# A decoder layer on one core: state and retrieval of its delta-rule recurrence in 32x32 blocks of TensorE

## The chip, the cores and the metric

The kernel runs on one core of a Trainium2 chip. The metric is the time of one execution on the device, in microseconds (us). Before the change the median of three runs is 969.68 us (969.55 to 969.97).

## The reference, cut to what matters

A pre-norm decoder layer over x of 8 x 512 x 256: first a recurrent ("delta rule") attention with 16 heads of 16 features, then attention over a context, then a feed-forward block with quantised activations (8 bits, scaled by the 0.995 quantile of the absolute values) and ternary weights. The change concerns the recurrence and, at the end, the second quantile.

```python
def step(S, inp):
    q_t, k_t, v_t, beta_t = inp
    retrieval = jnp.einsum('bhij,bhj->bhi', S, k_t)
    S = S + jnp.einsum('bhi,bhj->bhij', beta_t * (v_t - retrieval), k_t)
    o_t = jnp.einsum('bhij,bhj->bhi', S, q_t)
    return (S, o_t)
_, out_t = lax.scan(step, S0, (q, k, v, beta))
...
amax = jnp.maximum(jnp.quantile(jnp.abs(x), 1.0 - 0.005), EPS)
```

S is one 16 x 16 matrix for each of 8 batch rows and 16 heads, 128 matrices in all.

## The kernel before

**Stages.** After a start of some 40 us the recurrence runs in 32 chunks of 16 tokens (`CT`, `NCK`), until about 620 us; then the attention over the context, the feed-forward block's upper product, the second quantile (`quantile(1, ...)`) and the lower product. Everything is in one program, in which each engine's queue is written out by hand; semaphores tie them together. The steps of a chunk j appear in the order in which the `for j in range(NCK + 1)` loop of each engine calls them.

**The loop from chunk to chunk.** Within a chunk the update vectors of 16 tokens depend on each other. VectorE solves this triangular system (`solve(j, ...)`, some 30 small operations) and then transposes the update vectors (`updates_turned`, L1344, two halves, semaphore `ut_ready`). TensorE adds the chunk's outer products to the state (`state`, L1933). The state stays in one PSUM bank, `psS`, accumulated over all chunks. It is copied to SBUF, TensorE multiplies it with the keys and queries of the next chunk (`retrieval`, L1971, semaphore `ret_mm`), and VectorE starts the next chunk's right side from that (`start_chunk`, L1427) and solves again.

**Blocks and zeros.** A partition of these tiles is a batch row and a token (keys, updates) or a batch row and a feature (state). Every product is block-diagonal: 8 batch rows of 16 partitions. The 32x32 transposes of VectorE give tiles in which two batch rows share a 32-block; the kernel before spreads them into full 128x128 operands with zeros around the blocks:
- `keys_spread` on ScalarE (L725, four copies a chunk) spreads the turned keys `kt` into `kexp`, of which `state` takes 8 matrices of 128x128 as stationary operands against 64 columns each.
- `state` on ScalarE (L698, eight copies of 32 partitions, the lower two blocks, in two halves by heads, semaphore `sexp_act`) and `state` on VectorE (L1412, four masked products, the upper two blocks, `sexp_dve`) spread the state into `sexp`, of which `retrieval` takes one 128x128 matrix for each head, 16 in all, against up to 96 columns: 32 of its own head's and, on either side, columns that lie between and meet zeros in `padded`.

A matmul in f32 appears in the trace as two passes, each a weight load (PEld) and a matmul (PE); so `state` is 16 passes a chunk and `retrieval` 32. The word pass is used in this sense below.

**What stands between them on TensorE.** Between `state` and `retrieval` TensorE does a transpose of the next inputs (L2068), `values` (L2024) and `updates_turned` (L1943), 12 passes. After `retrieval` come the key sums (L2033), `far_gram` (L1956), `attention` in products of 32 rows by 128 columns (L1994), `outputs` in products of 128 rows by 32 columns (L2046), and then projections and the near grams, up to the next `state`.

**Who waits for what.** TensorE's sequencer executes a semaphore instruction of its own when a matmul has more waits than one; these appear in the trace as EVENT_SEMAPHORE (PEldq), at L1932 before `state` (for `ut_ready`) and at L2066 behind it (for the next transpose). ScalarE copies the attention products out (L733), which frees their banks.

**The second quantile.** `narrowed(1, ...)` compares 2048 candidates a partition with 4 edges: three marks by VectorE in bf16 (L1682), counted by TensorE (edges 0 and 2, L2282) and by ScalarE (edge 1, L1160), and the fourth marked and counted by VectorE alone (L1683). Then the candidates under a bound are kept: 1280 columns by VectorE (L1704), 768 by GpSimd (L682, L684), and VectorE takes the 8 largest of each 64 (L1709).

## Time and profile before

| | before |
|---|---|
| median of 3 runs | 969.68 us (969.55 to 969.97) |
| the profiled execution, its own time | 975.51 us |
| its span, first to last instruction | 973.6 us |
| TensorE (PE) busy | 861.1 us, 88% |
| VectorE (DVE) busy | 822.7 us, 85% |
| ScalarE (ACT) busy | 699.3 us, 72% |
| GpSimd (POOL) busy | 523.5 us, 54% |
| mean granted clock of TensorE | 0.950 of full speed |

PE is TensorE's matmuls, PEld its weight loads, and L12 is line 12 of the kernel. A row of the timeline is a group of like instructions in a row: when the first started, how long from there to the end of the last, and how many. The ends of matmuls are modelled and overlap the next start, so intervals between starts are used for how long a group holds TensorE. A granted clock of 1.00 is 2.4 GHz, and 0.50 is 1.2 GHz; a value between them is a mean over a stretch with both.

### The profile page before, as it was taken

The numbers are of one execution on the slowest core, as the hardware profiler recorded it, in microseconds if no ns is written. First come the engines' busy times: TensorE is split into PE (matmuls) and PEld (weight loads), VectorE is DVE, ScalarE is ACT, GpSimd is POOL, SyncE is SP. The second block draws the span as 40 slices with busy tenths as digits, with TensorE's granted clock in tenths as the row PEclk, the third lists the DMA queues.
The fourth block names the chain that finished last, engine by engine and source line by source line (L and its number), as shares of the span: only waits on it lengthen the run. The fifth ranks groups of instructions, "written<-read, shape, count | busy, mean of one in ns | idle before, by whom it ended". The sixth has DMA issues, their size and how long they took to land.

```text
span 973.6 us, 19722 instructions
## 1 busy us (share of the span) xinstructions
PE 861.1 (88%) x6257; PEld 657.5 (68%) x6257; DVE 822.7 (85%) x2508; ACT 699.3 (72%) x1819; POOL 523.5 (54%) x501
## 2 busy tenths in 40 slices
PE   7899999999999999999999999879999813995285
PEld 6687887787787787787787777556666513443264
DVE  4789999989999999999999988756777787899797
ACT  4688888887788788788778766536777750895095
POOL 5446656665465565565455544445888860980100
PEclk9899999999999999999999999989999965998599
DMA  9900000000000000004000000133110000000023
GB/s 162 159 1 13 7 7 13 6 7 12 7 8 11 8 7 11 8 7 140 8 8 10 9 6 8 36 132 130 66 66 0 2 1 0 1 1 1 0 68 106
DMA packets 28573, 30.50 MB, mean 31 GB/s; under 512 B 5548, under 2 KB 23864, under 8 KB 28472
## 3 DMA queue, kind: packets, MB, share of 16 engines
q1 hardware_dynamic: 28256, 29.12, 11.9%
q8 instruction: 51, 0.84, 0.4%
q14 instruction: 50, 0.41, 0.1%
q10 hardware_dynamic: 216, 0.14, 0.1%
HBM read 20.85 MB, written 4.19 MB: 26 GB/s over the span
## 4 chain that ended last, share of the span: by engine, by line
PE 65%; ACT 15%; DVE 12%; issue 6%; POOL 1%; DMA 1%; ACTq 0%; POOLq 0%; DVEq 0%
PE ps L2002 10%; PE ps L1933 5%; PE psY L1971 5%; PE psX L1971 4%; PE ps L2118 4%; PE psG L1956 4%; PE ps L1994 4%; ACT arena L733 3%; PE psG L1950 3%; PE ps L2060 3%; PE psX L2139 3%; PE psY L2139 2%; PE ps L2325 2%; PE psG L1951 2%; ACT arena L698 2%
## 5 line engine op out<-in xcount | busy, mean ns | idle before, releaser
L523 POOL TENSOR_SCALAR_AFFINE_SELECT arena<-arena 128x2048 f32<-128x2048 f32 x32 | 64.5, 2015 | 163.3 <-DVE arena L1308 163.3
L538 POOL TENSOR_TENSOR work<-work,half 128x16 f32<-128x16 f32 x32 | 94.9, 2966 | 2.7
L527 POOL TENSOR_SCALAR_AFFINE_SELECT arena<-arena 128x2048 f32<-128x2048 f32 x32 | 92.1, 2879 | 2.2
L698 ACT ACTIVATE arena<-ps,nparity 32x128 f32<-32x128 f32 x248 | 76.2, 353 | 18.8 <-PE ps L1933 17.3
L1994 PE MATMUL ps<-work 32*128 32x256 f32 x512 | 82.6, 402 | 3.0 <-ACT arena L733 2.9
L733 ACT ACTIVATE arena<-ps 128x512 f32<-128x512 f32 x128 | 69.3, 593 | 16.6 <-PE ps L1994 15.8
L1994 PEld LDWEIGHTS ps<-work 32*128 32x128 f32 x512 | 53.5, 184 | 37.3 <-issue 28.3
L1327 DVE TENSOR_REDUCE arena<-arena 128x64 f32<-128x256 f32 (+1 forms) x96 | 65.9, 687 | 3.3
L1971 PE MATMUL psY<-work,arena 128*128 128x96 f32 (+1 forms) x512 | 61.7, 280 | 3.1 <-ACT arena L698 2.0
L1971 PEld LDWEIGHTS psY<-work,arena 128*128 128x128 f32 x512 | 60.0, 196 | 6.5 <-issue 6.5
L537 POOL TENSOR_SCALAR work<-work 128x16 f32<-128x16 f32 x32 | 8.1, 254 | 102.1 <-ACT work L750 102.1
L1956 PE MATMUL psG<-arena 128*128 128x512 f32 x128 | 62.7, 612 | 0.0
L1933 PEld LDWEIGHTS ps<-work,arena 128*128 128x128 f32 x496 | 58.2, 192 | 5.2 <-issue 3.5
L1933 PE MATMUL ps<-work,arena 128*128 128x64 f32 x496 | 59.4, 273 | 0.5 <-DVE work L1344 0.5
L1971 PEld LDWEIGHTS psX<-work,arena 128*128 128x128 f32 x480 | 54.7, 192 | 4.6 <-issue 4.6
L1971 PE MATMUL psX<-work,arena 128*128 128x96 f32 (+1 forms) x480 | 56.3, 276 | 1.5 <-ACT arena L698 0.3
L2002 PEld LDWEIGHTS ps<-arena 128*128 128x128 f32 x384 | 48.1, 196 | 9.4 <-ACT arena L733 4.6
L1412 DVE TENSOR_TENSOR arena<-ps,arena 32x256 f32<-32x256 f32 x124 | 51.4, 414 | 3.5 <-PE ps L1933 1.2
L2002 PEld LDWEIGHTS ps<-nT,arena 128*128 128x128 f32 x384 | 46.3, 191 | 9.3 <-ACT arena L733 4.1
L2002 PE MATMUL ps<-arena 128*128 128x128 f32 x384 | 51.2, 284 | 0.9
L725 ACT ACTIVATE arena<-work 32x256 f32<-32x256 f32 x124 | 51.0, 411 | 1.1
L2002 PE MATMUL ps<-nT,arena 128*128 128x128 f32 x384 | 49.3, 279 | 2.1 <-ACT nT L787 1.2
(362 smaller groups left out, 2498.1 us busy)
## 6 DMA issues: line engine op xcount, KB each, us to landing
arena<-in_mask_BxSxS_ik SPq DMA_DIRECT2D x8, 1024.0 KB, 6.7
xs<-arena SPq DMA_DIRECT2D x256, 16.0 KB, 1.8
arena<-in_ctx SPq DMA_DIRECT2D x8, 512.0 KB, 4.2
out<-xs SPq DMA_DIRECT2D x32, 128.0 KB, 1.7
arena<-in_x SPq DMA_DIRECT2D x8, 288.0 KB, 17.5
arena<-in_L_ffn_w SPq DMA_DIRECT2D x2, 1024.0 KB, 20.6
arena<-in_x SPq DMA_DIRECT2D x16, 96.0 KB, 6.6
arena<-in_L_attn_w_qkvb SPq DMA_DIRECT2D x2, 512.0 KB, 5.9
```

The source lines that it names most:

```text
L523: G.affine_select(out=keys, in_=keys, compare_op=ALU.is_ge, fill=0.0, base=0, pattern=[[0, NH], [1, P]], channel_multiplier=-1).then_inc(h ...
L527: G.affine_select(out=pairs, in_=pairs, compare_op=ALU.is_ge, fill=0.0, base=0, pattern=[[0, NH], [-CT, B], [0, CT]], channel_multiplier=1 ...
L538: own(G.tensor_tensor(root, length, half, ALU.pow))
L698: last = A.activation(sexp[rows, heads, cols], psS[rows, :].rearrange("p (h n) -> p h n", n=32)[:, heads, HD * e:HD * e + HD], ACT.Copy, s ...
L733: A.activation(attn[j % 2][:, r * 512:(r + 1) * 512], ps[(2, 0)[r % 2]][:, :], ACT.Copy).then_inc(att_out, 1)
L1327: own(V.tensor_reduce(sums, part, AX.X, ALU.add))
L1412: last = V.tensor_tensor(sexp[rows, heads, 32 * r:32 * r + 32], psS[rows, :].rearrange("p (h n) -> p h n", n=32)[:, heads], block16[rows, ...
L1933: last = M.matmul(psS[:, b * 64:b * 64 + 64], kexp[:, b, :], utm[:, b * 64:b * 64 + 64], start=j == 0 and b == 0, stop=True, skip_group_ch ...
L1956: M.matmul(psG[:, f * 512:(f + 1) * 512], block16[:, :], PF[m % 2][:, f * 512:(f + 1) * 512], start=True, stop=True).then_inc(g1_mm, 1)
L1971: last = M.matmul(into[:, h - 1 + a:h - 1 + b], sexp[:, h, :], rows[:, h, a:b], start=False, stop=True, skip_group_check=True)
L1994: last = M.matmul(ps[(2, 0)[r % 2]][:, f * 2 * P:(f + 1) * 2 * P], kq[j % 4][rows, f * P:(f + 1) * P], qe[rows, f].rearrange("p e t -> p ( ...
L2002: last = M.matmul(out[:, f * P:(f + 1) * P], wq_s[:, c, first:first + P], nT[m % 4][:, c, :], start=c == 0, stop=c == DC - 1)
```

## The change

Everything below is in the new kernel; its line numbers differ from those of the kernel before.

- **State.** TensorE's `state` takes `kt` itself: for each of the 8 pairs of heads four products of 32 rows by 32 columns, one for each 32-block on the diagonal, against 64 columns. That is 32 matmuls in place of 8. `keys_spread` and `kexp` are gone. One product of zeros clears `psS` before the first chunk.
- **Copying the state.** ScalarE alone copies it, as it lies in PSUM, with the parity of the batch row as a scale: four copies of 128 partitions (16 columns x 8 heads), two for each half of the heads, semaphore `state_copied`. `state` on VectorE is gone.
- **Retrieval.** For each head four products of 32x32 against the head's own 32 columns: 64 matmuls in place of 16.
- **Turning keys.** `keys_turned` on VectorE moves behind `scale_near` and waits for `s_mm` in place of `kexp_ready`.
- **Second quantile.** VectorE marks all four edges in bf16, TensorE counts all four, and the sum of ScalarE and the part of GpSimd are gone; VectorE keeps all 2048 columns.
- GpSimd clears 512 columns in place of 3072 at the start.

```diff
             def state(j):
-                pe.wait_ge(kexp_ready, j + 1)
+                pe.wait_ge(kt_ready, j + 1)
+                if j == 0:
+                    pe.wait_ge(ut_ready, 1)
+                    M.matmul(psS[:, :], zeros[:, 0:P], zeros, start=True, stop=True)
                 for b in range(NH // 2):
                     if b % 4 == 0:
                         pe.wait_ge(ut_ready, 2 * j + 1 + b // 4)
-                    last = M.matmul(psS[:, b * 64:b * 64 + 64], kexp[:, b, :], utm[:, b * 64:b * 64 + 64],
-                                    start=j == 0 and b == 0, stop=True, skip_group_check=True)
+                    for r in range(4):
+                        rows = slice(32 * r, 32 * r + 32)
+                        last = M.matmul(psS[rows, b * 64:b * 64 + 64], kt[rows, b * 32:b * 32 + 32],
+                                        utm[rows, b * 64:b * 64 + 64], start=False, stop=True, skip_group_check=True)
...
                 for h in range(NH):
                     if h % (NH // 2) == 0:
-                        pe.wait_ge(sexp_dve, 2 * m - 1 + h // (NH // 2))
-                        pe.wait_ge(sexp_act, 2 * m - 1 + h // (NH // 2))
-                    a, b = 1 if h == 0 else 0, 2 if h == NH - 1 else 3
-                    last = M.matmul(into[:, h - 1 + a:h - 1 + b], sexp[:, h, :], rows[:, h, a:b],
-                                    start=False, stop=True, skip_group_check=True)
+                        pe.wait_ge(state_copied, 2 * m - 1 + h // (NH // 2))
+                    for r in range(4):
+                        rows = slice(32 * r, 32 * r + 32)
+                        last = M.matmul(into[rows, h], scopy[rows, h, :], streams[rows, h, 1],
+                                        start=False, stop=True, skip_group_check=True)
...
                 act.wait_ge(s_mm, j)
                 for heads in (slice(0, NH // 2), slice(NH // 2, NH)):
-                    for r in range(2, 4):
-                        rows = slice(32 * r, 32 * r + 32)
-                        for e in range(2):
-                            cols = slice(32 * r + HD * e, 32 * r + HD * e + HD)
-                            last = A.activation(sexp[rows, heads, cols],
-                                                psS[rows, :].rearrange("p (h n) -> p h n", n=32)[:, heads, HD * e:HD * e + HD],
-                                                ACT.Copy, scale=nparity[rows, e:e + 1])
-                    last.then_inc(sexp_act, 1)
+                    for e in range(2):
+                        cols = slice(HD * e, HD * e + HD)
+                        last = A.activation(scopy[:, heads, cols],
+                                            psS[:, :].rearrange("p (h n) -> p h n", n=2 * HD)[:, heads, cols],
+                                            ACT.Copy, scale=nparity[:, e:e + 1])
+                    last.then_inc(state_copied, 1)
...
             def keys_turned(m):
-                v.wait_ge(kexp_ready, m)
+                v.wait_ge(s_mm, m)
                 V.transpose(kt, kq[m % 4][:, 0:CW]).then_inc(kt_ready, 1)
...
-                    state(j + 1)
+                    if j + 1 < NCK - 1:
+                        keys_turned(j + 1)
...
-                n_own = (n_cand, KEPT_ON_DVE)[k]
-                own(V.scalar_tensor_tensor(cand2[:, 0:n_own], values[:, 0:n_own], bounds[:, 1:2], values[:, 0:n_own],
-                                           ALU.is_lt, ALU.mult))
+                own(V.scalar_tensor_tensor(cand2[:, 0:n_cand], values, bounds[:, 1:2], values, ALU.is_lt, ALU.mult))
```

TensorE from `state` to the end of `retrieval`, before (L1933 is the state, L1971 the retrieval; in brackets the semaphores waited for):

```order
L1933 MATMUL ps<-work,arena 128x64 [waits ut_ready,kexp_ready]
L1933 MATMUL ps<-work,arena 128x64 x3
L1933 MATMUL ps<-work,arena 128x64 [waits ut_ready]
L1933 MATMUL ps<-work,arena 128x64 x3
L2068 MATMUL ps<-ident,xn 128x128 [waits beta_ready,xn_ready]
...
L1971 MATMUL psY<-work,arena 128x64 [waits sexp_dve,sexp_act,dq_ready,k_ready]
L1971 MATMUL psY<-work,arena 128x96 x7
L1971 MATMUL psY<-work,arena 128x96 [waits sexp_act,sexp_dve]
L1971 MATMUL psY<-work,arena 128x96 x6
L1971 MATMUL psY<-work,arena 128x64
```

The same place in the changed kernel (L1890 is the state, L1928 the retrieval):

```order
L1890 MATMUL ps<-work 32x64 [waits ut_ready,kt_ready]
L1890 MATMUL ps<-work 32x64 x15
L1890 MATMUL ps<-work 32x64 [waits ut_ready]
L1890 MATMUL ps<-work 32x64 x15
L2025 MATMUL ps<-ident,xn 128x128 [waits beta_ready,xn_ready]
...
L1928 MATMUL psY<-work,arena 32x32 [waits state_copied,dq_ready,k_ready]
L1928 MATMUL psY<-work,arena 32x32 x31
L1928 MATMUL psY<-work,arena 32x32 [waits state_copied]
L1928 MATMUL psY<-work,arena 32x32 x31
```

The order of the steps is the same; there are four times as many matmuls in the two steps, and each half of the retrieval waits for one semaphore of ScalarE's in place of two engines'.

VectorE behind the transposed updates, before (L1420 turns the keys, L1358 and L1360 scale the near grams, L1412 spreads the state):

```order
L1344 STREAM_TRANSPOSE work<-arena 128x256 [waits s_mm,u_done]
L1344 STREAM_TRANSPOSE work<-arena 128x256
L1420 STREAM_TRANSPOSE work<-work 128x256 [waits kexp_ready]
L1339 TENSOR_TENSOR work<-work,ps 128x256 [waits kraw_ready,rn_T]
L1358 TENSOR_TENSOR arena<-psG,arena 128x512 [waits beta_ready,g2_mm]
L1360 TENSOR_TENSOR arena<-psG,arena 128x128x2
L1412 TENSOR_TENSOR arena<-ps,arena 32x8x32 [waits ret_mm,s_mm]
L1412 TENSOR_TENSOR arena<-ps,arena 32x8x32 x3
L1366 TENSOR_TENSOR arena<-psG,arena 128x128
```

And changed (L1319 and L1383 are the transposes of the updates and of the keys):

```order
L1319 STREAM_TRANSPOSE work<-arena 128x256 [waits s_mm,u_done]
L1319 STREAM_TRANSPOSE work<-arena 128x256
L1314 TENSOR_TENSOR work<-work,ps 128x256 [waits kraw_ready,rn_T]
L1333 TENSOR_TENSOR arena<-psG,arena 128x512 [waits beta_ready,g2_mm]
L1335 TENSOR_TENSOR arena<-psG,arena 128x128x2
L1383 STREAM_TRANSPOSE work<-work 128x256 [waits s_mm]
L1341 TENSOR_TENSOR arena<-psG,arena 128x128
```

The transpose of the keys now stands where the state was spread, behind the wait for `s_mm`.

## Rows read from the trace of the kernel before

**Rows 1.** Windows: stretch, us, busy PE, PEld, DVE, ACT, POOL, clock, DMA, GB/s.

```profile
328.00:344.00 16.00, 15.90 (x135) 12.52 (x135) 14.72 (x42) 13.11 (x37) 8.74 (x10) 1.00 0.04 10
```

**Rows 2.** Timeline of PE, 319 to 343 us: start, us, engine line, shapes, xpasses.

```profile
319.92 1.02 PE L1950 MATMUL psG<-arena 128*128 128x512 f32 x2
...
324.08 1.89 PE L1933 MATMUL ps<-work,arena 128*128 128x64 f32 x16
325.81 0.39 PE L2068 MATMUL ps<-ident,xn 128*128 128x128 f32 x2
...
327.40 3.76 PE L1971 MATMUL psX<-work,arena 128*128 128x64 f32 x32
330.99 0.56 PE L2033 MATMUL ps<-arena 128*128 128x8 f32 x4
...
342.35 1.91 PE L1933 MATMUL ps<-work,arena 128*128 128x64 f32 x16
```

**Rows 3.** Timeline of DVE, 322 to 345 us.

```profile
326.01 1.72 DVE L1412 TENSOR_TENSOR arena<-ps,arena 32x256 f32<-32x256 f32 x4
...
331.19 0.61 DVE L1427 SCALAR_TENSOR_TENSOR arena<-psX,columns,arena 128x128 f32<-128x128 f32 x2 [0.18 <-PE psX L1971]
...
341.70 0.77 DVE L1344 STREAM_TRANSPOSE work<-arena 128x256 f32<-128x256 f32 x2
```

**Rows 4.** Timeline of PE, a late chunk (idle before, and its releaser, in brackets).

```profile
601.07 1.97 PE L1933 MATMUL ps<-work,arena 128*128 128x64 f32 x16 [0.46 <-DVE work L1344]
```

**Rows 5.** Timeline of ACT, 322 to 345 us.

```profile
326.01 2.51 ACT L698 ACTIVATE arena<-ps,nparity 32x128 f32<-32x128 f32 x8 [0.50 <-PE ps L1933]
...
330.52 1.68 ACT L725 ACTIVATE arena<-work 32x256 f32<-32x256 f32 x4
```

**Rows 6.** The sequencer's semaphore at L1932, in the window 323.85 to 323.86 us.

```profile
L1932 PEldq EVENT_SEMAPHORE  x1: 51/51/51, 323.9 to 323.9; - x1
```

**Rows 7.** The sequencer's semaphore at L2066, in the window 324.21 to 324.22 us.

```profile
L2066 PEldq EVENT_SEMAPHORE  x1: 51/51/51, 324.2 to 324.2; - x1
```

**Rows 8.** Timeline of PE, 334 to 335.5 us: products of 32 columns, then of 32 rows.

```profile
334.37 1.08 PE L2046 MATMUL psY<-arena,work 128*32 128x128 f32 x32
335.38 0.48 PE L1994 MATMUL ps<-work 32*128 32x256 f32 x1
```

**Rows 9.** Waits of PE, 56 to 550 us: us in total, times, longest.

```profile
PE ps L1994 <- ACT arena L733: 1.0, 2, 0.5
```

**Rows 10.** Timeline of PE around the longest chunk, 543 to 565 us.

```profile
543.62 1.97 PE L1933 MATMUL ps<-work,arena 128*128 128x64 f32 x16
...
555.91 1.61 PE L1994 MATMUL ps<-work 32*128 32x256 f32 x8 [0.84 <-ACT arena L733]
...
564.55 1.89 PE L1933 MATMUL ps<-work,arena 128*128 128x64 f32 x16
```

**Rows 11.** Busy time and granted clock in two stretches, columns as in rows 1.

```profile
38.00:42.00 4.00, 4.00 (x13) 2.76 (x12) 3.62 (x15) 2.53 (x11) 0.40 (x1) 0.50 1.11 296
...
556.00:560.00 4.00, 4.00 (x19) 3.08 (x20) 3.66 (x11) 2.70 (x7) 0.00 (x0) 0.77 0.00 0
```

**Rows 12.** Timeline of PE and DVE in the first chunk.

```profile
35.16 2.36 PE L1994 MATMUL ps<-work 32*128 32x256 f32 x8 [1.06 <-ACT arena L733]
...
45.41 1.90 PE L1933 MATMUL ps<-work,arena 128*128 128x64 f32 x16
...
41.51 0.77 DVE L1344 STREAM_TRANSPOSE work<-arena 128x256 f32<-128x256 f32 x2
```

**Rows 13.** Timeline of DVE in the second quantile.

```profile
891.80 3.68 DVE L1682 TENSOR_SCALAR work<-work 128x2048 bf16<-128x2048 f32 x3
895.39 2.34 DVE L1683 TENSOR_SCALAR_CACHE_REDUCE work<-work 128x2048 uint8<-128x2048 f32 x1
...
899.24 1.54 DVE L1704 SCALAR_TENSOR_TENSOR work<-work 128x1280 f32<-128x1280 f32 x1
...
904.70 0.48 DVE L1709 MAX8 work<-work 128x8 f32<-128x64 f32 x3 [1.26 <-POOL work L684]
```

More of the change, by code:

```diff
@@ L278, in decoder @@
         edge_marks = cand2.bitcast(mybir.dt.uint8)
-        block_marks = [cand2[:, 0:FF].bitcast(BF16), cand2[:, FF:2 * FF].bitcast(BF16), gq[2][:, 0:2 * FF]]
-        last_marks = gq[2][:, 2 * FF:3 * FF].bitcast(mybir.dt.uint8)
-        KEPT_ON_DVE = 20 * KEPT
-        edges_counted = (EDGES, EDGES - 1)
+        block_marks = [half[:, k * 2 * FF:(k + 1) * 2 * FF] for half in gq[1:3] for k in range(2)]
+        edges_counted = (EDGES, 1)
         marks = [edge_marks[:, 4096 + 256 * e:4352 + 256 * e] for e in range(3)]
@@ L717, in updates_turned @@
                 last.then_inc(ust_ready, 1)
-            def keys_spread(j):
-                act.wait_ge(kt_ready, j + 1)
-                act.wait_ge(s_mm, j)
-                for r in range(4):
-                    rows = slice(32 * r, 32 * r + 32)
-                    last = A.activation(kexp[rows, :, 32 * r:32 * r + 32],
-                                        kt[rows, :].rearrange("p (b n) -> p b n", n=32), ACT.Copy)
-                last.then_inc(kexp_ready, 1)
             def attention_out(j, r):
@@ L1158, in _ @@
             act.wait_ge(picked, 2 * NT)
-            act.wait_ge(edge_marked, 2)
-            A.activation(block_marks[1], block_marks[1], ACT.Copy, accum_out=counts[:, 1:2]).then_inc(part[1], 1)
             act.wait_ge(found, 1)
@@ L2278, in quantile @@
                 if k == 1:
[L2279 removed]
+                    for e in range(EDGES):
                         pe.wait_ge(edge_marked, e + 1)
                         for c in range(2 * FF // P):
[L2282 removed]
+                            last = M.matmul(psY[:, e:e + 1], block_marks[e][:, c * P:(c + 1) * P], ones_b[:, 0:1],
                                             start=c == 0, stop=c == 2 * FF // P - 1)
```

68 lines of the change are left out of this document (18 added, 50 removed).

## The prediction

> **What bounds the kernel now.** I read busy time by windows first, then the timelines of TensorE, VectorE and ScalarE over one chunk, then the waits. In a stretch of 16 us TensorE is busy for 15.90, VectorE for 14.72 and ScalarE for 13.11, at the full clock [rows 1]. Thus TensorE looks like the bound, with little for the others' relief to give. The timelines show more. From one `state` to the next it is 342.35 - 324.08 = 18.27 us [rows 2]. In the late chunk where TensorE had less to do, it stood idle for 0.46 us before L1933 and was released by VectorE's transpose [rows 4]. In the ordinary chunk the transpose starts at 341.70 [rows 3] and L1933 at 342.35 [rows 2], so TensorE's own work and VectorE's solve end together. Both paths share one piece: from the start of `state`, 324.08, to the end of `retrieval`, after which `start_chunk` begins at 331.19 [rows 2, 3]. The reader should see this: the other 11 us of the chunk are covered twice, once by VectorE's solve and once by TensorE's other products, while these 7.1 us are in both. What `state` and `retrieval` lose or gain, the chunk loses or gains, 31 times.
>
> **Pace of the 128x128 passes.** `state` has 16 passes from 324.08 to 325.81, 0.108 us each; `retrieval` has 32 from 327.40 to 330.99, 0.112 us each [rows 2]. Passes of 64 and of up to 96 columns cost the same, so the full-width weight load paces them.
>
> **Pace of the 32x32 passes.** The trace has none. Two rows bound it. (a) Products of 32 output columns, four blocks side by side: 32 passes in 1.08 us, of which the last one's own length is some 0.27, so (1.08 - 0.27)/31 = 0.026 us each [rows 8]. They stream 128 columns; the new ones stream 64 and 32, and can be no slower for that. (b) How fast the sequencer can hand them out: between its semaphore at L1932 and that at L2066 lie the 16 passes of `state`, and the two fall in windows 0.36 us apart [rows 6, 7], 0.0225 us for each pass with its weight load. I take 0.024, between them, since neither run is as long as the new retrieval (128 passes) nor has tiles small in both directions.
>
> Here the Trainium skill speaks against the change: "TensorE: Matmul & The Clock Gate", section "Step-by-step: what each phase is for", says that with hardware decode off the sequencer's microcode spends about 62 ns on each MATMUL. By that rule, as an estimate, the 192 new passes would take 11.9 us a chunk and the sum would end about 200 us above the time before. By that rule 16 passes could not have gone out in 0.36 us, so the trace disagrees, and the row decides, for a run of this length.
>
> **The change, part by part, for a chunk.**
> - `state`: 8 x 4 matmuls, 64 passes x 0.024 = 1.54 us in place of 1.73: -0.19.
> - `retrieval`: 16 x 4 matmuls, 128 passes x 0.024 = 3.07 us in place of 3.59: -0.52.
> - Going into or out of a narrow shape. L2046 starts at 334.37 and the next product at 335.38, 1.01 us for 32 passes that at 0.026 take 0.83 [rows 8]: 0.18 lost at the change of shape. Four changes a chunk are new. The two ways in are mostly covered, because the sequencer hands passes out meanwhile; the two ways out are not: +0.36. (Bounds: one, +0.18, and four, +0.72.)
> - The wait for the copied state. Eight copies take 2.51 us [rows 5], so half of them 1.25, and the first half of the retrieval waits for four, until about 326.01 + 1.25 = 327.26, plus the way to TensorE: L1971 starts at 327.40. TensorE's own 12 passes between, from 325.81 at 0.11 each, end at 327.14. That is 0.26 us of waiting. After the change the first half needs two copies, 0.63 us, and is ready before TensorE: -0.26. A copy of 128 partitions has the same elements per partition (16 x 8) as one of 32, so I price it the same.
> - VectorE loses L1412, 1.72 us a chunk [rows 3], and the key transpose moves behind the wait for `s_mm`, at which L1412 stood. It needs this: without it VectorE would arrive at `start_chunk` when it does now, 0.18 us before the retrieval ends [rows 3], and any gain over that would stop there. With it there is room for 1.5 us.
> - ScalarE loses L725, 1.68 us, and four of the eight L698, 1.25 us. In an ordinary chunk this is at no one's edge: TensorE waited for its copies (L733) for 1.0 us in all between 56 and 550 us [rows 9]. Nothing for it there.
> - Sum: -0.19 - 0.52 + 0.36 - 0.26 = -0.61 us a chunk, x 31 = -19 us. With 0.0225 and one change of shape it is -0.29 - 0.71 + 0.18 - 0.26 = -1.08, -33 us; with 0.026 and four it is -0.07 - 0.26 + 0.72 - 0.26 = +0.13, +4 us.
>
> **Chunks that ScalarE lengthened.** The chunk from 543.62 to 564.55 takes 20.93 us, 2.7 over the others. TensorE waits 0.84 us for L733 in it [rows 10], and the clock then falls: 0.77 in the next 4 us [rows 11]. ScalarE comes 2.9 us sooner after the change, more than the wait; the pause and what follows go: -2.7. Two waits of 0.5 us between 56 and 550 [rows 9] go as well: -1. Together -3.7 (from 0 to -5).
>
> **The first chunk.** TensorE waits 1.06 us for L733, which stands behind L725, and then runs at 0.50 [rows 11, 12]; `state` starts at 45.41 although VectorE's transpose began at 41.51 [rows 12], some 3.3 us later than it could. With L725 gone most of this comes back; the new product of zeros costs about one L1950, 1 us [rows 2]. I take -2.5 (from 0 to -5). The shorter clearing on GpSimd lies beside the loading of inputs: 0.
>
> **The second quantile.** Three marks take 3.68 us and the fourth 2.34 [rows 13]; a fourth of the first kind takes 1.2, but the products and the copy behind it take back most, as far as the start of the same step: I take -0.3. Keeping 2048 columns in place of 1280 costs 1.54 x 768/1280 = +0.92, and the 1.26 us for GpSimd [rows 13] goes: -0.34. Together -0.6.
>
> **Sum.** -19 - 3.7 - 2.5 - 0.6 = -26 us against the profiled execution's 975.5 (span 973.6): 949.7. The median of the runs is 5.8 us below that execution, and the same difference from it gives 969.7 - 26 = **943.5 us**. The main case reaches from 969.7 - 33 - 5 - 5 = 926 to 969.7 + 4 - 0 - 0 - 0.3 = 973.
>
> **Rivals.**
> 1. *The clock falls behind the small tiles (slower).* The only fall inside the chunks comes after 3 us of narrow products with a pause of 0.84 us in them [rows 10, 11]. Of that chunk's 2.7 us over, 1.8 are not the pause but the slow passes behind it. After the change there are 1.5 and 3 us of passes that use a sixteenth of the array each, more narrow work at a stretch than now. Against it: L1994 and L2046 run in every chunk without a fall. If it falls once in each chunk, 31 x 1.8 = +56, net 999; once in every second, 971. It outweighs the gain from 26/1.8 = 14 or 15 falls on. Chance 0.20, and about a quarter of it ends below the time before.
> 2. *The small passes do not run side by side (slower).* No row shows tiles narrow both ways. Were each paced like the passes of L1933 now, 0.108 [rows 2], 192 of them would take 20.7 us in place of 5.3, +480 us; at 0.045, twice the sequencer's row, 8.6, and +3.3 us a chunk, about 1045. What speaks for it is only that the queue might be served from a store that the short run of 16 did not empty. The Trainium skill's 62 ns for a MATMUL is of this kind. Chance 0.10.
> 3. *Nothing gained in the blocks.* Pace 0.026 and four uncovered changes of shape, so that only the outer terms remain, 963 to 973. Chance 0.15; it counts half as faster and the rest as no change or slower.
> 4. *VectorE or ScalarE caps it.* At more than 1.5 us a chunk VectorE would be late for `start_chunk`. The sum doesn't reach that. Chance 0.03, time 920 to 926.
>
> The forecast has the remaining 0.52. A change within 0.2%, some 2 us, can't be told from none. Faster: 0.52 + 0.03 + 0.08 + 0.05 = 0.68; same 0.04; slower 0.28. The range runs from the fast end of the main case, 926, to 990, which takes in the milder half of rival 1 and leaves out its full form and rival 2.
>
> **What would show it.** In the profile after: `state` start to next start 1.5 to 1.8 us with 64 passes, `retrieval` 2.9 to 3.5 with 128; start of the retrieval no longer after a ScalarE row; chunks of 17.2 to 18.2 us; granted clock 1.00 in the windows from 60 to 600; VectorE at `start_chunk` still released by the retrieval; no 20.9 us chunk; the first `state` before 43.5 us. I am wrong if the passes stand 0.04 us or more apart, if the clock row shows less than 1.00 in windows where it was 1.00, or if chunks shrink by more than 1.2 us.

## The result and the profile after

| | before | after |
|---|---|---|
| median | 969.62 us (968.35 to 969.97, 4 runs) | 936.63 us (932.97 to 938.91, 4 runs) |
| ratio | | 0.9659, 95% interval 0.9626 to 0.9692 |
| the profiled execution, its own time | 975.51 us | 935.96 us |
| its span | 973.6 us | 934.1 us |
| TensorE / VectorE / ScalarE busy | 861.1 / 822.7 / 699.3 us | 789.1 / 781.6 / 600.1 us |
| mean granted clock | 0.950 | 0.935 |

The change is faster by 33 us, 3.4%. Every ratio here is of a kernel's runs within 1.5% of its fastest; two of the four runs of experiment 6, its profiled one among them, and one of experiment 11 lie outside. The forecast was 943.5 us (926 to 990). The size is near, but the account below has other entries than the prediction's.

The same stretch as in [rows 1], by windows of the profile after (us; busy PE, PEld, DVE, ACT, POOL; clock; DMA share; GB/s):

```profile
328.00:344.00 16.00, 14.67 (x257) 10.64 (x245) 15.03 (x40) 11.68 (x35) 8.74 (x8) 1.00 0.05 11
```

In this stretch VectorE is now the busiest engine. TensorE's timeline of an ordinary chunk after, to hold beside [rows 2] (L1890 is the state, L1928 the retrieval, L1990 the key sums):

```profile
310.92 1.10 PE L1890 MATMUL ps<-work 32*32 32x64 f32 x64 [0.35 <-DVE work L1319]
311.95 0.44 PE L2025 MATMUL ps<-ident,xn 128*128 128x128 f32 x2
...
313.43 1.29 PE L1928 MATMUL psX<-work,arena 32*32 32x32 f32 x128
315.36 0.61 PE L1990 MATMUL ps<-arena 128*128 128x8 f32 x4 [0.64 <-DVE arena L1379]
...
327.26 1.09 PE L1890 MATMUL ps<-work 32*32 32x64 f32 x64 [0.22 <-DVE work L1319]
```

The chunk is 327.26 - 310.92 = 16.34 us, where it was 18.27. TensorE waits for VectorE before the state and before the key sums; between 56 and 550 us this adds up, and there is a new kind of wait, in the middle of the retrieval (columns: us in all, times, longest):

```profile
PE ps L1990 <- DVE arena L1379: 11.9, 18, 3.0
PE ps L1890 <- DVE work L1319: 9.9, 18, 1.3
PE psX L1928 <- issue: 8.7, 11, 1.8
PE psY L1928 <- issue: 6.4, 9, 2.5
```

"issue" means that TensorE waited for nothing that the profile shows. Two such pauses on TensorE's timeline (178.25 and 435.30), and between them the long chunk in which VectorE also makes the ternary factors:

```profile
178.25 0.32 PE L1928 MATMUL psX<-work,arena 32*32 32x32 f32 x15 [1.82 <-issue]
...
239.48 1.09 PE L1890 MATMUL ps<-work 32*32 32x64 f32 x64
...
246.77 1.02 PE L1990 MATMUL ps<-arena 128*128 128x8 f32 x4 [2.98 <-DVE arena L1379]
...
261.09 1.10 PE L1890 MATMUL ps<-work 32*32 32x64 f32 x64
...
435.30 0.66 PE L1928 MATMUL psY<-work,arena 32*32 32x32 f32 x53 [2.46 <-issue]
```

Behind such pauses the clock often falls, though not behind the first of these. Windows after, with the clock before the last two columns:

```profile
176.00:180.00 4.00, 2.18 (x73) 1.55 (x62) 3.31 (x11) 2.13 (x8) 3.16 (x5) 1.00 0.03 7
180.00:184.00 4.00, 4.00 (x51) 2.60 (x49) 3.66 (x11) 3.94 (x10) 3.69 (x5) 1.00 0.09 21
...
244.00:248.00 4.00, 1.23 (x5) 1.23 (x6) 3.91 (x12) 0.19 (x3) 1.25 (x2) 0.72 0.08 16
248.00:252.00 4.00, 4.00 (x8) 1.38 (x9) 3.27 (x11) 2.03 (x7) 3.58 (x3) 0.50 0.09 21
...
436.00:440.00 4.00, 4.00 (x10) 1.73 (x12) 3.58 (x14) 2.14 (x7) 3.11 (x2) 0.62 0.11 26
```

TensorE ahead of the first `state` ([rows 12]; L1884 is the product of zeros), and VectorE in the second quantile ([rows 13]; L1643 the marks, L1659 and L1661 the keeping):

```profile
38.26 2.05 PE L1907 MATMUL psG<-arena 128*128 128x512 f32 x2
...
43.87 1.02 PE L1884 MATMUL ps<-arena 128*128 128x512 f32 x2
44.83 1.09 PE L1890 MATMUL ps<-work 32*32 32x64 f32 x64
```

```profile
853.13 4.88 DVE L1643 TENSOR_SCALAR work<-work 128x2048 bf16<-128x2048 f32 x4
...
860.27 2.34 DVE L1659 SCALAR_TENSOR_TENSOR work<-work 128x2048 f32<-128x2048 f32 x1
862.64 4.15 DVE L1661 MAX8 work<-work 128x8 f32<-128x64 f32 x32
...
867.52 0.48 DVE L1676 TENSOR_SCALAR_CACHE_REDUCE work<-work 128x256 uint8<-128x256 f32 x1
```

So the 39.5 us between the two profiled spans come about as follows. Start to first `state`: 45.41 to 44.83, -0.6. The 30 periods from the first to the last `state`: 555.66 (45.41 to 601.07) became 520.21 (44.83 to 565.04), -35.5. Last `state` to the second quantile's marks: 290.73 to 288.09, -2.6. The second quantile, marks to the next count: 15.25 to 14.39, -0.9. The rest, 66.55 to 66.58. The 35.5 divide again: 30 x (18.27 - 16.35) = -57.6; the former excess over 18.27, 7.6 us, is gone; and after has 29.7 us over 30 x 16.35, of which 22.8 lie in five chunks of 22.5, 22.0, 21.6, 18.9 and 19.5 us, and most of the rest in eight chunks of 17.1 to 17.2. In each of the five the clock falls to 0.50: in the first behind a wait of 1.56 us and in the third behind one of 2.98 us for VectorE (L1379), in the other three behind idle times marked issue of 1.83, 1.75 and 2.46 us.

The profiled execution of the kernel before was itself 6 us longer than its median, so that 39.5 is more than 33: its clock fell in two chunks. One fall stands behind the first `state`, where TensorE had run full-width passes alone since 37.45 us and then waited for 1.47 us (clock 0.69 in the window):

```profile
49.22 5.38 PE L1971 MATMUL psY<-work,arena 128*128 128x64 f32 x32 [1.47 <-ACT arena L698]
...
48.00:52.00 4.00, 2.78 (x15) 2.81 (x15) 3.91 (x10) 3.90 (x14) 0.00 (x0) 0.69 0.00 0
```

The other is the chunk of [rows 10]. In experiment 1, whose recurrence is unchanged, there is no fall between 44 and 600 us, these two chunks are 18.76 and 19.20 us in place of 20.38 and 20.92, and the 30 periods are 551.84 us. Against that the change took 31.6 us.

**Three questions follow:** what sets 16.35, what makes the chunks of some 17.15, and what makes the five long ones.

### The profile page after: what moved, and what is told of

The parts are those of the page before. It is cut to its first block, busy times and chain, and to the rows that moved or that the text cites. A ratio compares the mean times of both kernels' runs of the same rounds, so it can differ in the third digit from the quotient of the medians.

```text
span 934.1 us, 28216 instructions
## 1 busy us (share of the span) xinstructions
PE 789.1 (84%) x10755; PEld 564.5 (60%) x10755; DVE 781.6 (84%) x2383; ACT 600.1 (64%) x1569; POOL 518.8 (56%) x498
## 4 chain that ended last, share of the span: by engine, by line
DVE 46%; PE 39%; issue 8%; ACT 5%; POOL 1%; DVEq 0%; ACTq 0%; POOLq 0%
PE ps L1959 5%; DVE arena L1294 5%; DVE arena L1302 4%; PE ps L2075 4%; DVE arena L1366 3%; PE psG L1913 3%; PE psX L2096 3%; DVE arena L1280 3%; DVE arena L1376 3%; DVE arena L1283 3%; PE psY L2096 2%; PE ps L1951 2%; PE ps L2282 2%; PE psG L2075 2%; DVE arena L1275 2%
## 5 line engine op out<-in xcount | busy, mean ns | idle before, releaser
L2075 PE MATMUL ps<-arena,nT 128*128 128x512 f32 x84 | 42.6, 631 | 6.9 <-issue 4.5
L758 ACT ACTIVATE arena<-ps,columns 128x128 f32<-128x128 f32 x64 | 20.0, 363 | 43.1 <-PE ps L1959 43.1
L1119 ACT ACTIVATE arena<-ps,small 128x512 f32<-128x512 f32 x64 | 41.7, 689 | 6.6 <-PE ps L2282 5.7
L948 ACT ACTIVATE arena<-arena 128x512 f32<-128x512 f32 x32 | 23.1, 721 | 32.9 <-DVE arena L1431 32.8
L1890 PE MATMUL ps<-work 32*32 32x64 f32 x1984 | 34.0, 215 | 11.7 <-DVE work L1319 11.4
L1890 PEld LDWEIGHTS ps<-work 32*32 32x32 f32 x1984 | 29.6, 105 | 23.3 <-issue 23.3
L1280 DVE TENSOR_TENSOR arena<-arena 128x128 f32<-128x128 f32 x128 | 38.8, 303 | 4.4
L1294 DVE TENSOR_TENSOR arena<-psG,arena 128x1024 f32<-128x1024 f32 x32 | 39.2, 1224 | 1.6 <-PE psG L1913 0.4
L1283 DVE TENSOR_REDUCE arena<-arena 128x32 f32<-128x128 f32 x128 | 36.6, 286 | 4.4
L2282 PE MATMUL ps<-work 128*128 128x512 bf16 x128 | 38.1, 379 | 1.5 <-ACT work L1114 1.5
```

Of the source, the lines that this page charges most:

```text
L1280: own(V.tensor_tensor(part, g3h[:, :, a].rearrange("p h (t s) -> p h t s", s=4), C16[:, :, 4 * a:4 * a + 4].rearrange("p h (a s) -> p h a ...
L1283: last = V.tensor_reduce(C16[:, :, t:t + 2], part, AX.X, ALU.add)
L1294: mult = V.tensor_tensor(part, src, C16[:, :, t - n:t].rearrange("p h (a s) -> p h a s", a=1).broadcast_to([P, NH, n, n]), ALU.mult)
L2075: last = M.matmul(logit_bank(n), nT[n % 2][:, c, :], ctxT[b % 2][:, c, :], start=c == 0, stop=c == DC - 1)
```

## The experiments

Since the clock falls in other chunks from one profile to the next, the length of ordinary chunks, from one `state` to the next at the full clock, is the finer measure; the total time then tells what the falls cost.

**1. The second quantile alone.** The kernel before with only that part of the change.

> The kernel before with only the second quantile changed (four marks in bf16 by VectorE, all counted by TensorE, 2048 columns kept by VectorE). The prediction priced this at -0.6 us: a time of 969, a ratio of 0.9994, nothing a measurement can tell from no change. If the second quantile carries part of the gain that the blocks were not given, the ratio is below 0.998.

Measured: 969.96 us, ratio 0.9978 (0.9946 to 1.001). Its marks start at 886.67 and the same next count at 901.07, 14.40 us against 15.25: -0.85, as after. The interval of the total can't tell this from zero; the rows can.

**2. The state alone.**

```diff
-                    last = M.matmul(psS[:, b * 64:b * 64 + 64], kexp[:, b, :], utm[:, b * 64:b * 64 + 64], ...)
+                    for r in range(4):
+                        rows = slice(32 * r, 32 * r + 32)
+                        last = M.matmul(psS[rows, b * 64:b * 64 + 64], kt[rows, b * 32:b * 32 + 32],
+                                        utm[rows, b * 64:b * 64 + 64], start=False, ...)
```

> The kernel before with only TensorE's state in 32x32 blocks; the state is still spread by VectorE and ScalarE and the retrieval still multiplies 128x128. Theory A (the narrow passes are much quicker than forecast, but VectorE's own work sets the chunk): VectorE keeps its 1.72 us and arrives at start_chunk when it did, 0.18 us before the old end of the retrieval, so at most 0.18 us a chunk is gained, 6 us in all: 962 to 968, with TensorE standing idle before start_chunk's products instead. Theory B (TensorE's path sets the chunk and the state gives back its 0.7 us whole): 31 x 0.7 = 22 us, 948. Theory C (narrow passes bring the clock down): granted clock below 1.00 in windows of the recurrence where it was 1.00, and a time above 970.

Measured: 965.93 us, ratio 0.9941 (0.9902 to 0.9981), chunks of 18.2 us, clock 1.00 in every window from 56 to 600 us. Theory A holds. Most of the state's 0.7 us turns into a wait of some 0.6 us for VectorE's spreading of the state (L1401 here), in 27 chunks between 56 and 550 us:

```profile
336.75 1.10 PE L1927 MATMUL ps<-work 32*32 32x64 f32 x64
...
339.93 2.33 PE L1965 MATMUL psY<-work,arena 128*128 128x64 f32 x19 [0.60 <-DVE arena L1401]
```

**3. The retrieval alone**, with the copy by ScalarE alone, and the state still 128x128.

> The kernel before with only the retrieval in 32x32 blocks and the state copied by ScalarE alone; the keys are still spread and the state still takes 128x128 matrices. Theory A (VectorE sets the chunk after the change): VectorE has as little work as in the changed kernel, the slower state is hidden, and the time is that of the changed kernel or up to 3 us more, 935 to 941. Theory B (TensorE's path sets it): the state's 0.7 us a chunk is missing, 937 + 22 = 958. Theory C (instruction supply): the run of 128 passes still has idle times in its middle, but fewer than in the changed kernel, since the state issues a quarter of the matmuls; Theory D (the clock falls because of narrow passes): fewer and shorter stretches below 1.00 than in the changed kernel, and for that reason alone a time a few us below it.

Measured: 951.18 us (945.80 to 957.34), ratio 0.9793 (0.9731 to 0.9855). The shortest chunks are 16.3 to 16.7 us, many others without a long pause 16.8 to 17.0, so the retrieval and VectorE's 1.72 us make most of the gain of a chunk. The time is neither A's nor B's, since six falls of the clock took much of the gain back. Theory C holds by count, seven idle times marked issue for seventeen after, but they are of 1.1 to 2.3 us each. Theory D fails: two thirds of the narrow passes, and more falls. Three of the six stand behind idle times marked issue (1.56, 2.26, 1.19 us) and three behind waits for ScalarE's attention copies (L732: 1.39, 0.71, 1.75 us); ScalarE still spreads the keys here, and the changed kernel has no such wait. The worst chunk, of 24.3 us, with a full-width state ahead:

```profile
255.08 1.89 PE L1919 MATMUL ps<-work,arena 128*128 128x64 f32 x16
...
261.76 0.18 PE L1957 MATMUL psY<-work,arena 32*32 32x32 f32 x1 [2.26 <-issue]
...
279.42 1.89 PE L1919 MATMUL ps<-work,arena 128*128 128x64 f32 x16
```

The clock falls here without the narrow state, and every one of the falls has an idle time of TensorE just ahead of it.

**4. Work behind the retrieval.**

```diff
+            def filler():
+                M.matmul(psS[:, 0:256], ones[:, :], zeros[:, 0:256], start=False, stop=True, ...)
...
                     retrieval(j)
+                    filler()
```

> The changed kernel with one full-width matmul of 256 columns (two passes, some 0.5 us), which adds zeros to the state's bank, behind each retrieval, where TensorE waits for VectorE's products anyway. Theory D (the long chunks come from clock falls, and these from too little work of the array around the narrow passes): granted clock 1.00 from 60 to 600 us, the three stretches with chunks of 19 to 22 us are gone, 937 - 20 = 917 at best. Theory E (the falls follow from the idle times in the middle of the retrieval, or from the slow start, and filler behind it changes nothing): the stretches stay, 935 to 940. If the filler itself stands on the path: 31 x up to 0.5 us more, up to 952.

Measured: 924.08 us (920.42 to 931.70), ratio 0.9496 (0.9458 to 0.9533), clearly under the changed kernel's. The filler costs nothing that shows, since it stands where TensorE waited: the ordinary chunks are still 16.35 us. In the profiled execution, the longest of its runs, the first two chunks are 16.4 and 19.3 us in place of 22.5 and 22.0. The idle times inside the retrieval stay (1.81, 1.88, 1.80 us), with a fall behind each, and the chunk with VectorE's factors is 24.9 us. So neither D nor E alone: the filler shortens some pauses and can't reach those ahead of it.

**5 and 6. VectorE's work, more and less.** One more transpose of the keys; or one product (L1379) given to GpSimd.

```diff
                 v.wait_ge(s_mm, m)
+                V.transpose(sexp_flat[:, 1024:1280], kq[m % 4][:, 0:CW])
                 V.transpose(kt, kq[m % 4][:, 0:CW]).then_inc(kt_ready, 1)
```

> The changed kernel with one more transpose of the keys on VectorE in each chunk (0.36 us start to start, into columns nobody reads), in front of the one that is there. Theory A (VectorE's own work sets the ordinary chunk): every chunk grows by 0.36 us, 31 x 0.36 = 11 us, 948, and the waits of TensorE for VectorE before the state grow by as much. Theory B (TensorE's path through state and retrieval sets it): the transpose lies beside it, 937 to 939, and start_chunk is released by the retrieval.

> The changed kernel with the third near product (L1379, 128 columns, 0.20 us start to start) taken from VectorE and given to GpSimd for chunks 2 and later. Theory A (VectorE sets the ordinary chunk): 30 x 0.2 = 6 us less, 931. Theory B (TensorE's path sets it): no gain, 935 to 939. If GpSimd's product comes too late for the near gram, or slows VectorE beside it, the chunk grows and the time is above 940.

More: 938.34 us, ratio 0.9652 (0.9604 to 0.9699). The total would speak for theory B, but it had three falls where the changed kernel had five. The chunks decide: none of 16.35 is left, nearly all are 17.0 to 17.2.

```profile
501.03 1.10 PE L1891 MATMUL ps<-work 32*32 32x64 f32 x64 [0.84 <-DVE work L1319]
...
518.20 1.09 PE L1891 MATMUL ps<-work 32*32 32x64 f32 x64 [0.84 <-DVE work L1319]
```

Less: 932.93, 939.89, 952.72 and 953.48 us, ratio 0.9644 (0.958 to 0.9709) of the first two, which shows nothing in the total; the profile is of the last, with six falls. Its shortest chunks, five of the 30, are 286.93 - 270.78 = 16.15 us, 0.2 under the changed kernel's shortest:

```profile
270.78 1.10 PE L1902 MATMUL ps<-work 32*32 32x64 f32 x64
...
286.93 1.10 PE L1902 MATMUL ps<-work 32*32 32x64 f32 x64
```

Most of its other short chunks are 16.26 to 16.32 us; there L1361, the same operation as L1351 below, takes 0.41 us in place of 0.28. Both agree with A: VectorE sets the chunk. But 0.36 us of work made 0.8 us of chunk, which A doesn't explain. VectorE's rows do, in the changed kernel itself, beside GpSimd's. A chunk of 16.34 us, then one of 17.17 us:

```profile
315.22 0.28 DVE L1351 TENSOR_TENSOR arena<-arena 128x128 f32<-128x128 f32 x1
...
331.70 0.81 DVE L1351 TENSOR_TENSOR arena<-arena 128x128 f32<-128x128 f32 x1
```

```profile
315.28 0.80 POOL L582 TENSOR_TENSOR arena<-arena 128x256 f32<-128x256 f32 x1
...
331.64 0.72 POOL L582 TENSOR_TENSOR arena<-arena 128x256 f32<-128x256 f32 x1
```

Where L1351 starts 0.06 us ahead of GpSimd's addition it takes 0.28 us; where it starts 0.06 us behind, 0.81. In the changed kernel it takes 0.50 to 0.81 us in seven of the eight chunks of 17.1 to 17.2 us and 0.27 to 0.28 in all the others; the eighth, from 172.8 us, holds the idle time of 1.82 us. The added transpose makes it late in most chunks: its mean between 80 and 560 us is 580 ns there and 373 in the changed kernel. The Trainium skill says as much ("SBUF — State Buffer", section "Who interferes with whom"): a VectorE instruction with two SBUF inputs contends with a GpSimd instruction that reads SBUF, and the order of issue decides which of the two blocks. The rows agree: the late one ends at 332.51 us, 0.15 behind GpSimd's addition.

**7. Columns of zeros**, as in the kernel before: up to 96 columns for each product of the retrieval.

> The changed kernel with the retrieval's 64 products streaming 96 columns in place of 32, the neighbours' columns of zeros among them, as the kernel before did. Theory F (the columns that four blocks side by side stream set the pace: 64 columns in 0.016 us and 32 in 0.009 us a pass so far): some 0.02 us a pass, the retrieval takes 2.6 us from start to start in place of 1.2. Theory G (something for each pass, weight load or hand-out, sets it): 1.2 to 1.4 us as now. For the time: if the 1.4 us more lie in the room before start_chunk, 935 to 941; and if the idle times in the middle of the retrieval come from passes that are used up faster than they are supplied, these shrink, the clock falls that follow them are fewer, and the time may be below the changed kernel's, 925 to 935. If they lie on the path, 31 x 1.4 = 43 us more, 980.

Measured: 931.12 us (929.47 to 937.24), ratio 0.9611 (0.9561 to 0.9661). Theory F is right on the pace:

```profile
318.32 2.73 PE L1929 MATMUL psY<-work,arena 32*32 32x64 f32 x128
320.99 0.61 PE L1991 MATMUL ps<-arena 128*128 128x8 f32 x4
```

2.67 us from start to start, 0.021 us a pass. TensorE itself now sets chunks of 17.0 us, where 16.35 were possible, and still the kernel is not slower than the changed one (the two intervals overlap): only four idle times marked issue above 0.3 us are left between 56 and 575 us, where there were seventeen, and the clock is 1.00 in every window from 40 to 560 us, in spite of pauses of 1.87 and 2.05 us. So a pause of this length behind narrow passes need not bring the clock down.

**8. Work in the middle of the retrieval.**

```diff
                     if h % (NH // 2) == 0:
                         pe.wait_ge(state_copied, 2 * m - 1 + h // (NH // 2))
+                        if h > 0:
+                            filler()
```

> The changed kernel with the full-width matmul of 256 columns between the two halves of the retrieval in place of behind it. Theory H (a burst of 128 quick passes uses up the instructions that are at hand, and the idle times marked issue are the wait for more): the filler gives 0.5 us of supply in the middle, the idle times of 1.7 to 2.5 us in the retrieval become shorter or rarer than the three to five there are now, and the clock falls behind them go; 915 to 925. If supply comes at a fixed place whatever the pace (theory I), the idle times stay as they are, and the time is that of the kernel with the filler behind the retrieval, 920 to 930. If the filler delays start_chunk: 31 x 0.1 to 0.4 us more than that.

Measured: 924.89 us (921.12 to 933.30), ratio 0.9547 (0.9479 to 0.9615). Theory H: seven idle times in the retrieval above 0.3 us, the longest 1.20 us, and between 56 and 560 us one fall only, in the chunk of 24.9 us where VectorE makes the factors.

What supplies the passes? The queue "q8 instruction" moved 71 packets of 16 KB between 60 and 600 us in the changed kernel, 36 before. In the changed kernel and experiments 3, 4, 7, 8 and the last one, every one of the 55 idle times above 0.3 us marked issue in or behind a retrieval ends 2.2 to 2.9 us after a packet of this queue starts. For instance, the changed kernel's packet at 175.6 us (its DMA in a window of 0.2 us) and the row of 178.25 above:

```profile
DMA packets 1, 0.02 MB, mean 82 GB/s; under 512 B 0, under 2 KB 0, under 8 KB 0
...
q8 instruction: 1, 0.02, 41.3%
```

The reading that fits is that TensorE used up its instructions and waited for the next block: the idle times end within the same 0.7 us behind a packet, and they grow rarer when the passes are slower or interrupted. No view shows the store of instructions itself. The Trainium skill ("Runtime: NRT & Kernel Launch", section "Instruction fetch mechanics") says that instructions are fetched in blocks of 16 KiB while the current one is executed, and that this is hidden because instructions are dispatched more slowly than blocks arrive. The block size agrees with the packets; that it is hidden does not hold, on this reading, for passes 0.0095 us apart, with idle times of up to 2.5 us.

**9. A pause in the kernel before**: nine transposes more on VectorE ahead of the near products of two chunks.

> The kernel before, with nine more transposes on VectorE (some 0.4 us each, 3.6 us) in front of the near products of chunks 14 and 22, so that TensorE, behind its full-width state and retrieval, stands still before the key sums for about 3 us, as it does once in the changed kernel. Theory J (a pause of TensorE of some 2 us or more brings the clock down whatever went before it): the clock falls behind both pauses, and the two chunks grow by more than the pause, to about 24 us or more. Theory K (it takes the pause and the narrow passes ahead of it): the clock stays at 1.00 and the two chunks are 18.3 + 3 = 21.3 to 22 us.

Measured: 988.44 us (two runs, 986.12 and 990.75), ratio 1.0176 (1.0139 to 1.0214); the two chunks are 29.7 and 24.7 us. Theory J:

```profile
267.96 3.76 PE L1974 MATMUL psY<-work,arena 128*128 128x64 f32 x32
275.43 1.02 PE L2036 MATMUL ps<-arena 128*128 128x8 f32 x4 [3.71 <-DVE arena L1407]
276.30 3.76 PE L1959 MATMUL psG<-arena 128*128 128x512 f32 x4
```

```profile
272.00:276.00 4.00, 0.57 (x3) 0.58 (x3) 3.79 (x11) 0.73 (x2) 0.00 (x0) 0.83 0.11 25
276.00:280.00 4.00, 4.00 (x8) 1.46 (x7) 3.38 (x13) 2.31 (x7) 3.16 (x2) 0.50 0.02 5
```

A pause of 3.71 us, twice, brings the clock down to 0.50 without any 32x32 pass. It is longer than those of the changed kernel, so it doesn't show that 1.8 us alone would do. The wait of 1.47 us in the first chunk of the kernel before, with a fall behind it, is as short as theirs; but there the clock had come up to 1.00 only 7 us earlier, so it is not quite their case.

**10. GpSimd's order.**

```diff
                 mask_attention(j)
+                if j + 3 < NCK:
+                    key_norms(j + 3)
                 pool.wait_ge(xr_ready, j + 1)
                 G.tensor_tensor(xc[:, j, :], xc[:, j, :], bb_s, ALU.add).then_inc(xb_ready, 1)
                 if j >= 1:
                     x_added(j - 1)
-                if j + 3 < NCK:
-                    key_norms(j + 3)
```

> The changed kernel with GpSimd's two additions of 256 columns (L582, L543) moved behind its key norms. Theory L (chunks take 17.15 us in place of 16.35 where VectorE's L1351, 0.28 us when alone, falls behind GpSimd's L582 and takes 0.8, and L1280 takes 0.47 for 0.29): L1351 takes 0.28 in every chunk, the ordinary chunks are all 16.3 to 16.4 us, and about a dozen chunks lose 0.8 us each, -10 us beside whatever the clock falls do, so about 927. Theory M (the 17.15 us chunks come from the idle times in the middle of the retrieval): they stay.

Measured: 930.27 us (928.22 to 939.70), ratio 0.9610 (0.9567 to 0.9652). Theory L: L1351 takes 278 ns on average, L1353 394 in place of 628, and 21 of the 30 chunks are 16.3 to 16.5 us and none is 17.1 or 17.2, though the idle times marked issue are still there, thirteen above 0.3 us. So those of 0.4 to 0.9 us were not what made 17.15. The 30 periods are 512.44 us, 7.8 less than in the changed kernel; 21.9 us over 30 x 16.35 are left, most of it in the chunks of the six falls.

```profile
L1353 DVE TENSOR_TENSOR arena<-arena 128x128 f32<-128x128 f32 x29 | 11.4, 394 | 1.0
...
L1351 DVE TENSOR_TENSOR arena<-arena 128x128 f32<-128x128 f32 x29 | 8.1, 278 | 0.0
```

**11. Together**: the filler in the middle, GpSimd's order, and five fillers behind the retrieval of chunk 12.

> The changed kernel with the filler between the halves of the retrieval, five more fillers (some 2.2 us) behind the retrieval of chunk 12, where VectorE's ternary factors keep TensorE waiting, and GpSimd's additions behind its key norms. If pauses of TensorE behind narrow passes cause the clock falls: granted clock 1.00 from 60 to 560 us and no chunk above 20 us; 925 - 6 for chunk 12, - 10 for the chunks of 17.15 us: 909. If theory L is wrong, 918. If the fillers of chunk 12 don't hold the clock, that chunk stays at 24.9 us, 915.

Measured: 920.48 us (912.42 to 926.53), ratio 0.9448 (0.9415 to 0.9481), not the 909. Chunk 12 fell from 24.9 to 18.5 us with the clock at 1.00, and the ordinary chunks are 16.35; but pauses of 1.14 and 1.28 us for instructions still had a fall behind them (chunks of 19.0 and 21.6 us), while one of 1.45 us had none.

**12. 64 columns**, GpSimd's order, and three fillers behind the retrieval of chunk 12.

```diff
-                    for r in range(4):
-                        rows = slice(32 * r, 32 * r + 32)
-                        last = M.matmul(into[rows, h], scopy[rows, h, :], streams[rows, h, 1],
+                    a, b = (0, 2) if h == NH - 1 else (1, 3)
+                    for r in range(4):
+                        rows = slice(32 * r, 32 * r + 32)
+                        last = M.matmul(into[rows, h - 1 + a:h - 1 + b], scopy[rows, h, :], streams[rows, h, a:b],
```

> The changed kernel with the retrieval's 64 products streaming 64 columns, their own 32 and 32 of a neighbour's zeros, with GpSimd's additions behind its key norms, and three fillers behind the retrieval of chunk 12. With 32 columns the retrieval takes 1.2 us from start to start and TensorE then waits some 0.9 us a chunk; with 96 it takes 2.67 and TensorE itself sets chunks of 17.0. If columns set the pace, 64 give 128 x 0.0155 = 2.0 us, which fits into the wait: chunks of 16.3 to 16.4 us, idle times marked issue rarer and shorter than with 32 columns, granted clock 1.00 almost throughout: 908 to 914, the fastest version of these. If the idle times stay as with 32 columns: 920 to 930. If TensorE sets the chunk already at 64 columns, chunks of 16.7 and 922.

Measured: 912.24 us (909.46 to 918.86), ratio 0.9386 (0.9363 to 0.9408), the fastest of all and the only one whose interval lies under those of both 4 and 11.

```profile
312.25 1.09 PE L1890 MATMUL ps<-work 32*32 32x64 f32 x64
...
314.75 1.99 PE L1929 MATMUL psY<-work,arena 32*32 32x64 f32 x128
317.09 0.61 PE L1991 MATMUL ps<-arena 128*128 128x8 f32 x4 [0.35 <-DVE arena L1379]
...
328.59 1.09 PE L1890 MATMUL ps<-work 32*32 32x64 f32 x64
```

The retrieval is 0.70 us longer than with 32 columns (1.29); the waits before the state and the key sums, 0.35 and 0.64 us in the changed kernel's chunk, are 0.35 together; and the chunk stays at 16.34 us. Between 56 and 550 us TensorE's waits are down to 15.0 us in all from 36.9, and two short falls are left (clock 0.61 and 0.58 in one window of 4 us each). Which share is due to the columns, to GpSimd's order and to the three fillers was not separated.

## Why the prediction was right in size, and where its steps failed

- **What bounded the kernel** was read rightly: from the start of `state` to `start_chunk` the two engines share a piece. It was 6.91 us (324.08 to 330.99, [rows 2]) and is 2.51 us (310.92 to 313.43) and some 1.21 for the retrieval, 3.7 in all: TensorE's part lost 3.2 us. Of this 0.1 is the wait for the copied state, forecast at 0.26.
- **The pace was mis-sized, and this is the step that failed**: "I take 0.024, between them". The row of [rows 8] was an upper bound, for passes of 128 columns, and the value was put beside it. The number of columns streamed sets the pace where four blocks lie side by side: 0.026 us at 128 (that row, with products of 128 rows by 32), and with the 32x32 products 0.021 at up to 96 (experiment 7), 0.016 at 64 (`state`, 1.03/64) and 0.0095 at 32 (in experiment 4 the retrieval starts at 232.70 and the filler behind it at 233.91, 1.21/128). The pace falls with the columns, though not in proportion. The lower bound of 0.0225, from the sequencer's semaphores [rows 6, 7], was none: the new passes go faster than that, and the same two semaphores of the changed kernel (L1887 and L2023) stand at 310.81 and 311.59 us, 0.78 us for 64 passes, 0.012 each. What spaced them by 0.36 us before is not shown. So `state` gave -0.70 (forecast -0.19) and `retrieval` -2.38 (forecast -0.52); no term for the change of shape can be seen.
- **The 62 ns a MATMUL** of the Trainium skill ("TensorE: Matmul & The Clock Gate", section "Step-by-step: what each phase is for") was rightly set aside: the trace has 0.0095 us a pass. Rival 2 is out.
- **VectorE's cap, rival 4**, was seen ("At more than 1.5 us a chunk") and given 0.03; it is what happened, at 1.92 us. The room was L1412's 1.72 and the 0.18 that VectorE had waited before `start_chunk` [rows 3], 1.90 in all, where "room for 1.5 us" was put. Experiments 2, 5 and 6 show it. Had the pace been read as set by columns, the cap would have been the main case, at 1.5 x 31 = 46 us, and with the outer terms the forecast 969.7 - 46 - 6.8 = 917: nearer for the chunk, and 20 us too fast in total (33 with the 1.9 measured).
- **Rival 1, the clock**, happened in part: five falls, not one in each chunk, and for another reason. Narrow products left the clock at 1.00 with little pause (experiment 2) and even with two pauses of some 2 us (experiment 7), and a pause brought it down without 32x32 passes (experiment 9, and 1.47 us in the first chunk of the kernel before). That "The only fall inside the chunks" came behind narrow products [rows 10, 11] was misread: there were two, the other at 49.5 us behind that wait. The price was too low: the five chunks cost 22.8 us over 16.35, 4.6 each, pauses included, where 1.8 was put.
- **Three things were in no term**: idle times marked issue inside the retrieval, VectorE's L1351 beside GpSimd, and TensorE's waits for VectorE before the key sums, long enough in two chunks for a fall of the clock. All gave back part of a gain that was itself three times the forecast's: -57.6 for the chunks where the sum had -19, and 30 us returned. That 936.6 lies near 943.5 is owed to errors that cancel.
- **Chunks lengthened by ScalarE, -3.7**: right for the profiled execution; the chunk of 20.9 us [rows 10] is gone and so is TensorE's wait for the copies. But the sum carried it over to the median whole, while 1.7 of the 2.7 us are a fall that experiment 1, at 970.66 us, does not have (19.20 in place of 20.92 us).
- **The first chunk, -2.5**: wrong, -0.6, and not even that is sure: in experiment 1, without this part of the change, the first `state` starts at 44.06 us. It stands behind TensorE's own work, which runs without a pause from 38.26 to 44.83 us, until 41.0 at the low clock, with 0.96 us for the product of zeros; that VectorE's transpose was ready early [rows 12] was not a sign of idle time to be had back.
- **The second quantile, -0.6**: -0.86, in two kernels. The marks gave -0.3 as put (6.77 to 6.47 us up to the copy of the summed counts), the keeping -0.56 where -0.34 was put.
- **The -2.6 us between the last `state` and the quantile** hold the 31st of the shared pieces, which the sum counted with the chunks. From the last `state` to the far gram it was 6.99 us (601.07, [rows 4], to 608.06) and is 5.43 (565.04 to 570.47), an idle time of 1.69 marked issue included: -1.6. The rest was not traced; the clock falls behind that at differing places. The stretch is 290.0 to 291.7 us in the kernel before and experiments 1 to 3 and 9, and 287.3 to 291.0 in the runs with the whole change. The far gram, before and after:

```profile
608.06 1.94 PE L1956 MATMUL psG<-arena 128*128 128x512 f32 x4
...
570.47 1.99 PE L1913 MATMUL psG<-arena 128*128 128x512 f32 x4
```

**Still open:** why a pause of 1.82 us (178 us) or of 2.05 (experiment 7) leaves the clock alone and one of 1.28 (experiment 11) doesn't; and whether GpSimd's order alone would be worth something in the kernel before, which wasn't tried.

## What to carry to other kernels

When passes get shorter, ask who was one step behind: here another engine took over after 1.9 of 3.2 us, and the rest became pauses. Pauses on TensorE are not free even off the critical path, since the clock may fall behind them; fill them with harmless wide products, or make the quick passes a little longer than they need be, as long as that fits into the wait. For the cost of narrow passes, take a row with the same number of columns streamed, since fewer columns were quicker here at each step from 96 to 64 to 32; and compare kernels by their undisturbed periods before comparing totals.

## What the runs showed of the hardware that was not expected

- Four 32x32 blocks side by side: 0.021, 0.016 and 0.0095 us a pass in f32 at up to 96, at 64 and at 32 columns streamed; four of 128 rows by 32 took 0.026 at 128.
- A run of 128 such passes of 32 columns seems to outrun the supply of instructions: idle times of 0.3 to 2.5 us that end 2.2 to 2.9 us after a 16 KB packet starts. With 96 columns four were left of seventeen.
- An instruction of VectorE with two SBUF inputs took 0.81 us in place of 0.28 when it started 0.06 us behind an addition of GpSimd's.
- The clock fell to 0.50 behind pauses of 3.71 and, early on, 1.47 us in full-width work, and behind pauses of 1.1 to 3.6 us in the changed kernel and its variants, though not behind each: 1.82 and 2.05 us left it at 1.00.
